# Moving two soft products between two down tiles in the expert stage of a gated cross-attention layer

## The reference: what is computed

```
scores = softmax(x @ gate_w.T);  keep the top 8 of 64 per token  -> flat[n, g, 8]
scalar = flat.sum(-1)
soft = softmax(where(flat == 0, -1e9, flat))          # 8 shares per token and group
xg = x + soft @ mask_up[g].T                          # 512 features
g_ = xg @ gate_proj[g].T;  u_ = xg @ up_proj[g].T     # 352 inner columns
a = silu(g_) * u_;  d = a @ down_proj[g].T
y = sum over g of scalar[:, g] * d[:, g]
x = x + tanh(g_ffn) * y
```

## Time and profile before

| | before |
|---|---|
| median of 3 runs | 1072.21 us |
| the profiled execution | 1073.4 us, span 1071.6 us |
| PE busy | 1050.9 us, 98% |
| DVE busy | 747.2 us, 70% |
| POOL busy | 615.1 us, 57% |
| ACT busy | 389.5 us, 36% |
| granted TensorE clock, mean | 0.997 |

### The profile page before, as it was taken

How to read it: one execution, slowest core, us unless ns; L and a number is a source line. 1 busy time by engine, 2 the same in 40 slices (tenths; PEclk the granted TensorE clock), 3 DMA queues, 4 the chain that set the end, 5 groups by cost and what they waited for, 6 DMA issues and landing times.

```text
span 1071.6 us, 14530 instructions
## 1 busy us (share of the span) xinstructions
PE 1050.9 (98%) x5388; PEld 891.6 (83%) x5388; DVE 747.2 (70%) x1336; ACT 389.5 (36%) x651; POOL 615.1 (57%) x546
## 2 busy tenths in 40 slices
PE   8999999999999999999999999999999999999998
PEld 7889988988887778888877788888888888888886
DVE  7774665676567887797789898765666665666655
ACT  5333324334333444334425342333333333332331
POOL 0212102122334966777778888768677777668661
PEclk9999999999999999999999999999999999999999
DMA  9112225255776341114234443493311211221202
GB/s 334 69 41 99 60 50 148 61 140 136 237 246 191 122 39 59 62 57 54 87 113 41 129 126 104 140 320 115 113 61 60 74 42 60 74 74 47 74 28 79
DMA packets 114134, 111.65 MB, mean 104 GB/s; under 512 B 20880, under 2 KB 96400, under 8 KB 114064
## 3 DMA queue, kind: packets, MB, share of 16 engines
q1 hardware_dynamic: 113696, 110.58, 35.6%
q10 hardware_dynamic: 368, 0.15, 0.1%
HBM read 79.05 MB, written 31.65 MB: 103 GB/s over the span
## 4 chain that ended last, share of the span: by engine, by line
PE 84%; DVE 10%; issue 2%; POOL 2%; DMA 1%; ACT 1%; SPq 0%; DVEq 0%; ACTq 0%
PE bank L83 45%; PE bank L1660 32%; PE bank L1666 4%; PE bank L1491 2%; PE bank L1674 1%; DVE a_stack L1332 1%; DMA x2l<-ot_lo 1%; POOL wgu_lo L659 1%; DVE tmp L1341 1%; DVE a_stack L1330 1%; DVE a_tmp L1324 1%; DVE tmp L1454 1%; DVE xres L1348 1%; DVE tmp L1367 1%; DVE tmp L1449 0%
## 5 line engine op out<-in xcount | busy, mean ns | idle before, releaser
L1660 PE MATMUL bank<-x2t,wgu_hi 128*128 128x512 f32 x1144 | 353.0, 390 | 0.0
L659 POOL TENSOR_TENSOR wgu_lo<-wgu_raw,wgu_hi 128x512 fp32r<-128x512 f32 (+2 forms) x144 | 215.6, 1508 | 88.3 <-ACT wgu_hi L810 86.8
L1660 PEld LDWEIGHTS bank<-x2t,wgu_hi 128*128 128x128 f32 x1144 | 214.9, 188 | 44.2
L1660 PE MATMUL bank<-x2t,wgu_lo 128*128 128x512 f32 x572 | 224.6, 393 | 3.1 <-DVE a_tmp L1321 2.1
L810 ACT CAST wgu_hi<-wgu_raw 128x512 fp32r<-128x512 f32 (+1 forms) x129 | 93.7, 727 | 224.2 <-PE bank L1666 187.2
L1348 DVE TENSOR_TENSOR xres<-xres,bank 128x512 f32<-128x512 f32 x176 | 120.2, 683 | 50.6 <-PE bank L83 49.9
L83 PE MATMUL bank<-wd_hi,at_second 128*128 128x512 f32 x336 | 130.8, 389 | 0.0
L1660 PEld LDWEIGHTS bank<-x2t,wgu_lo 128*128 128x128 f32 x572 | 107.4, 188 | 27.2 <-DVE a_tmp L1321 3.4
L631 POOL TENSOR_TENSOR kt_lo<-ctxt_raw,kt_hi 128x256 fp32r<-128x256 f32 x32 | 23.5, 764 | 140.3 <-ACT kt_hi L835 140.3
L1341 DVE TENSOR_TENSOR tmp<-tmp,scalars 128x512 f32<-128x512 f32 x88 | 99.3, 1129 | 3.8 <-DMA scalars<-scals 0.8
L83 PE MATMUL bank<-wd_hi,at_first 128*128 128x512 f32 x256 | 99.9, 390 | 0.4 <-issue 0.4
(11 more groups left out here) (216 smaller groups left out, 2258.7 us busy)
## 6 DMA issues: line engine op xcount, KB each, us to landing
wgu_raw<-in_w_gate_up SPq DMA_DIRECT2D x43, 512.0 KB, 4.1
wd_raw<-in_w_down SPq DMA_DIRECT2D x22, 512.0 KB, 4.9
a_stacks<-a_stack SPq DMA_DIRECT2D x22, 192.0 KB, 1.9
a_stack<-a_stacks SPq DMA_DIRECT2D x22, 192.0 KB, 4.0
ctxt_raw<-in_ctx_t SPq DMA_DIRECT2D x8, 512.0 KB, 11.2
ctx_raw<-in_ctx SPq DMA_DIRECT2D x8, 512.0 KB, 8.4
x<-x_raw SPq DMA_DIRECT2D x8, 512.0 KB, 11.3
sums_raw<-x SPq DMA_DIRECT2D x16, 256.0 KB, 3.8
```

The source lines that it names most:

```text
L659: last = nc.gpsimd.tensor_tensor(wgu_lo[:, part], raw_of(quad)[:, part], f32(wgu_hi[:, part]), ALU.subtract)
L1660: last = nc.tensor.matmul(out_bank[:], stationary, moving, start=begins and n == 0, stop=n == len(pairs) - 1, skip_group_check=True)
```

## The change

In quads 3 to 21 TensorE issues the two soft products behind the first early down tile instead of ahead of it. In the same quads VectorE adds the first down tile ahead of c22, since c22 needs the soft product m5. Other quads are as they were, and no instruction is added or removed.

```diff
+def soft_between(q):
+
+    return early_tiles(q) == 2 and q < QUADS // 2
...
+                if soft_between(q):
+                    add_down(below)
                 dve.wait_ge(s_s3, q + 1)
                 dve.wait_ge(s_m5, q + 1)
                 nc.vector.tensor_tensor(sums[:, SUM_3], sums[:, SUM_3], psum_c[:], ALU.add).then_inc(s_c22, 1)
...
-                for n in range(early):
+                for n in range(1 if soft_between(q) else 0, early):
                     add_down(below + n)
...
                 product_7(quad)
-                soft_products(quad)
+                if not soft_between(q):
+                    soft_products(quad)
                 for n in range(early):
+                    if n == 1 and soft_between(q):
+                        soft_products(quad)
                     if n == 1 and q == 4:
                         pe.wait_ge(s_centre, B)
```

## The result

The changed kernel takes 1077.34 us, the median of 12 runs (1074.88 to 1083.79), against 1071.62 us for the kernel before (12 runs, 1070.23 to 1076.22). The ratio is 1.0053, with a 95% interval of 1.0035 to 1.0071: 5.7 us slower. The forecast was 1072.0 us, no change, with a range up to 1075.8. It was wrong: the kernel became slower, and the time lies above the range.

What follows compares the result with a forecast made beforehand. TensorE, busy 98% of the span, was taken as the bound. Its losses of 5.06 us would become 4.9 us, -0.2 us: 1073.2 us, carried to the median 1072.0 us; range for 8 in 10 1069.0 to 1075.8 us.

Steps and rivals of the forecast that it cites:

- The gain: TensorE's soft products stop waiting for a_stack, as the first down tile gives 1.36 us of cover: 4.4 us won.
- All seven losses: TensorE's lost time by the starts in quads 4, 8, 12, 15, 16, 17 and 19: 4.4 us, all to vanish.
- VectorE's edit at nothing: Adding the first down tile ahead of c22 on VectorE costs nothing; product_3's wait for c22 keeps 1.1 us of cover.
- The way from c11 to the down tile: Later c11 delays silu, group B's rounding and GpSimd's at_lo; down tiles in quads 12, 14, 16, 18 wait 0.7 to 1.5 us.
- I take 0, as holds are both gained and lost: GpSimd's 15 us runs against VectorE's port lock: net stretch 0, bounded by 3.9 us either way.
- The rival of one more hold in each run: GpSimd meets one more VectorE hold in each of quads 11, 13, 15, 17: 3.9 us more, 1075.9 us; chance 0.12.
- the forecast -0.2: Sum over TensorE's quads: losses of 5.06 us before become 4.9 us after, so nothing; chance 0.55.
- no case reaches: No forecast case reaches about 0.5%, 5.4 us, on either side; within 0.5% had chance 0.95.
- slipping a_tile: VectorE's a_tile slips by what TensorE gains, the soft pair waits again: 1073.8 us; chance 0.08.
- whole gain: GpSimd's run has hidden slack or its piece sums don't matter; 4.4 us go, nothing returns: 1067.8 us; chance 0.12.
- quads 4, 8 and 20 had no wait for at_lo: GpSimd's idle time swallows the delay: quads 4 and 8 keep 0.05 us loss each, quad 20 gets nothing back.
- GpSimd's idle time ahead of group B: Sign of being right: this idle time grows by up to 1.36 us, and those into quads 4 and 20 shrink.

Runs made afterwards that it cites:

- the late silu alone: The kernel before the change, but in quads 3 to 21 ScalarE's gate silu also waits for the first early down tile: 1078.67 us, ratio 1.0055.
- The first experiment: The changed kernel, but in quads 3 to 21 ScalarE rounds group B of the next quad's weights ahead of the silu waiting for c11: 1068.7 us, ratio 0.9968.
- the swap on ScalarE: Group B rounded ahead of the silu in quads 3 to 21: on the kernel before, 1071.63 us, ratio 0.9992; on the changed kernel, 1068.7 us.

## Why the prediction was wrong, point by point

**The gain: right.** All seven losses went. The losses of 4.4 us by the starts are 0 after, but for 0.1 us in quads 4 and 8.

**VectorE's edit at nothing: right.** Its old order gives the same distances. Product_3 never waited for c22.

**The way from c11 to the down tile: right in its mechanism.** Silu, rounding of group B, GpSimd's run, at_lo, down tile: quads 12, 14, 16 and 18 wait and no others do, and the late silu alone makes the same waits. The size was off. I had 1.2, 1.5, 1.4 and 0.7 us and they are 1.88, 1.85, 1.81 and 1.30, together 6.8 instead of 4.8 (6.4 if one counts only up to the first matmul). The step that failed is "I take 0, as holds are both gained and lost". From the start of group B's low part in quad 11 to the end of at_lo, GpSimd's run took 14.54 us before and 15.14 us after. The sums and the low part of group C in the changed kernel:

```profile
523.72 0.74 POOL L653 TENSOR_TENSOR wgu_raw<-wgu_raw 128x256 f32<-128x256 f32 x1
524.41 1.19 POOL L654 TENSOR_TENSOR wgu_raw<-wgu_raw 128x256 f32<-128x256 f32 x1
525.57 1.19 POOL L656 TENSOR_TENSOR wgu_raw<-wgu_raw 128x256 f32<-128x256 f32 x1
526.83 0.74 POOL L658 TENSOR_TENSOR wgu_raw<-wgu_raw 128x256 f32<-128x256 f32 x1
527.54 1.74 POOL L664 TENSOR_TENSOR wgu_lo<-wgu_raw,wgu_hi 128x512 fp32r<-128x512 f32 x1
```

and in the kernel before:

```profile
525.49 0.74 POOL L649 TENSOR_TENSOR wgu_raw<-wgu_raw 128x256 f32<-128x256 f32 x1
526.19 0.73 POOL L651 TENSOR_TENSOR wgu_raw<-wgu_raw 128x256 f32<-128x256 f32 x1
527.00 1.07 POOL L653 TENSOR_TENSOR wgu_raw<-wgu_raw 128x256 f32<-128x256 f32 x1
528.19 1.60 POOL L659 TENSOR_TENSOR wgu_lo<-wgu_raw,wgu_hi 128x512 fp32r<-128x512 f32 x1
```

Two sums of 0.74 us became 1.19 us, the third of those shown fell from 1.07 to 0.74, and the low part rose from 1.60 to 1.74: holds are indeed gained and lost, but not evenly. The rival of one more hold in each run had 3.9 us for this; it was 2.0 us over the four runs, half of that. That rival's 1075.9 us lies nearest to the result, but its one term makes only 2.0 of the 7.5 us, so the nearness is luck.

**What GpSimd's lateness does to VectorE: missed.** I had the holds only as a stretching of GpSimd's run. The lock works both ways. In quads 3, 8 and 12 VectorE's rows are lengthened by 0.6 to 0.7 us (in quad 3 by 0.66 us and 0.38 us). In quad 12 it is this row, before (first) and after, where GpSimd's group B runs from 540.64 to 542.48:

```profile
542.13 0.73 DVE L1185 TENSOR_TENSOR stack_tok<-soft,stack_tok 128x128 fp32r<-128x128 f32 x1
```

```profile
541.21 1.42 DVE L1190 TENSOR_TENSOR stack_tok<-soft,stack_tok 128x128 fp32r<-128x128 f32 x1
```

The residual adds come late, and in quads 4, 9 and 13, where TensorE must have all of them before it reuses bank 7, this costs 0.92, 0.69 and 0.66 us. With 0.8 us in quads 17 and 19 at a_masked, behind VectorE's long row L1357 (2.35 us in quads 16 and 18, where L1352 took 1.69 and 1.59 before), it is 3.1 us. Only the term of quad 3 has an experiment of its own. The first experiment takes the others away together, but for 0.41 us in quad 9 and 0.16 us in quad 17; that each comes from the lengthened row is read from the rows. The Trainium skill (SBUF — State Buffer, Who interferes with whom) states the lock for both engines, and the trace agrees; the prediction used only one side of it.

**SyncE's queue: missed.** I had looked at quad 20 only for at_lo, where the delay is indeed swallowed. But SyncE loads the weights of quad 22 when GpSimd's group C of quad 20 is done, and the token blocks of the second pass stand behind that load in the same queue. This costs 2.7 us in the profile of the changed kernel and 0.5 to 1.5 us in the others that have the delay.

The sum closes: the forecast -0.2, and 2.0 + 3.1 + 2.7 missed, is 7.6 us against 7.5 measured between the slots. The claim that "no case reaches" 0.5% rested on cases that followed only one of GpSimd's three consumers; the measured change is 0.53%, with an interval of 0.35% to 0.71%. The "slipping a_tile" and the "whole gain" did not occur as whole cases, and quads 4, 8 and 20 had no wait for at_lo, as forecast. Of the signs, GpSimd's idle time ahead of group B grew by 1.32 us in quad 3 and 1.36 us in quad 13, and that into quad 20 fell from 3.54 to 1.80 us; that into quad 4 stayed at 5.24 us, where it was to fall. The prediction speaks of ten even quads; from 4 to 20 there are nine, and nothing hangs on it.

## What to carry to other kernels

When a moved instruction releases something, go through all of the in-order queues behind that release, not only to the first place where the delay is swallowed: here one semaphore held a ScalarE row, that row held 15 us of GpSimd, and this held a down tile, VectorE's port and a transfer queue. A move that gains on the bounding engine may need a second one that keeps the other engines' release times; the swap on ScalarE cost nothing and turned 5.7 us of loss into 3.4 us of gain. Where two engines that do no matmuls lock each other out, a shift of one is not neutral by default; here VectorE was busy for 87% and GpSimd for 95% of the window of the earlier trace rows.

## What was not expected of the hardware

A VectorE operation of only 16 columns (L1174, one tile read in SBUF) was held by a GpSimd operation from 0.33 to 0.99 us, and one of 128 columns from 0.67 to 1.36 us in quad 8. VectorE's sums of 128x512 with an operand in PSUM took 0.67 to 0.69 us each throughout the first pass, before and after. And the profile's idle time for a TensorE wait was 0.24 to 0.28 us short of what the starts show (quad 12 after the change: 1.64 against 1.88 us).
